# A two-layer vision tower on one core: three unsplit patch blocks, value rows torn 16, 16 and 5, and a reordered tail

## The reference

```python
h = patches @ W_lin.T + b_lin; h = concat(class_token, h) + position   # 768 -> 256
h = h + attention(layernorm(h))      # 16 heads of 64, softmax with a relative bias
h = h + moe(layernorm(h))            # 7 experts (256 -> 1024 -> 256), top 2, one shared expert
# last layer
d = sigmoid(x @ W_delta.T + b_delta); v = x @ W_value.T + b_value      # x = layernorm(h)
state = (1 - d) * state + d * v      # along the 37 tokens;  h = h + state
r = sigmoid(mix_r(x) @ W_r.T); k = square(relu(mix_k(x) @ W_k.T))      # x = layernorm(h)
h = h + r * (k @ W_v.T)              # mix: mu * x + (1 - mu) * previous token
```

## Time and profile before

| | us |
|---|---|
| median of three runs | 309.29 |
| the profiled execution | 307.67 |
| its span, first to last instruction | 305.6 |
| PE busy | 297.2 |
| DVE busy | 191.0 |
| ACT busy | 187.3 |
| POOL busy | 154.7 |

### The profile page before, as it was taken

The page is one execution under the profiler, slowest core; times in us unless marked ns, Lnnn a source line. Parts: engine busy times, 40 slices in busy tenths (PEclk is TensorE's granted clock), DMA queues, the critical chain, the costliest instruction groups (busy, mean ns, idle before and its releaser), DMA issues.

```text
span 305.6 us, 7417 instructions
## 1 busy us (share of the span) xinstructions
PE 297.2 (97%) x3100; PEld 277.3 (91%) x3100; DVE 191.0 (63%) x368; ACT 187.3 (61%) x327; POOL 154.7 (51%) x142
## 2 busy tenths in 40 slices
PE   8999998999999999989999999999999999998995
PEld 7778788999999999979999999999999999985673
DVE  2694445657727868675828674755748686736962
ACT  4586335776636883546777676657576463678561
POOL 7043523666415151729577594967685785000333
PEclk9999999999999999999999999999999999999999
DMA  7979343554604332478674838384857652000002
GB/s 267 412 161 233 67 113 94 182 143 124 194 8 135 82 111 72 166 214 283 228 216 151 252 124 288 96 290 135 274 170 233 207 186 73 11 4 1 0 0 84
DMA packets 32432, 46.49 MB, mean 152 GB/s; under 512 B 6965, under 2 KB 18837, under 8 KB 32394
## 3 DMA queue, kind: packets, MB, share of 16 engines
q1 hardware_dynamic: 29994, 42.16, 44.3%
q0 software_dynamic: 960, 2.43, 2.4%
q10 hardware_dynamic: 1440, 1.38, 1.5%
HBM read 38.22 MB, written 5.71 MB: 144 GB/s over the span
## 4 chain that ended last, share of the span: by engine, by line
PE 91%; DVE 4%; DMA 2%; ACT 1%; issue 1%; SPq 0%; ACTq 0%; POOL 0%; DVEq 0%; POOLq 0%
PE ps L1708 22%; PE ps L1710 22%; PE ps L1709 22%; PE ps L2098 6%; PE ps L1880 3%; PE ps L1723 3%; PE ps L1730 2%; PE ps L1860 2%; PE ps L1716 2%; DMA v_region<-v_region 2%; PE ps L1845 2%; PE ps L1738 1%; DVE c_region L1129 1%; PE ps L2009 1%; PE ps L1973 1%
## 5 line engine op out<-in xcount | busy, mean ns | idle before, releaser
L1708 PE MATMUL ps<-c_region,w_hi 128*128 128x224 f32 (+2 forms) x304 | 88.3, 290 | 1.1 <-DVE c_region L1129 0.8
L1710 PE MATMUL ps<-c_region,w_lo 128*128 128x224 f32 (+2 forms) x304 | 85.4, 281 | 0.0
L1709 PE MATMUL ps<-c_region,w_hi 128*128 128x224 f32 (+2 forms) x304 | 85.2, 280 | 0.0
L572 POOL TENSOR_TENSOR w_lo<-w_stage,w_hi 128x512 fp32r<-128x512 f32 x30 | 47.4, 1600 | 33.9 <-ACT w_hi L847 33.9
L1708 PEld LDWEIGHTS ps<-c_region,w_hi 128*128 128x128 f32 x304 | 58.1, 191 | 2.6 <-DVE c_region L1129 1.4
L1709 PEld LDWEIGHTS ps<-c_region,w_hi 128*128 128x128 f32 x304 | 58.1, 191 | 0.3
L1710 PEld LDWEIGHTS ps<-c_region,w_lo 128*128 128x128 f32 x304 | 58.0, 191 | 0.0
L847 ACT ACTIVATE w_hi<-w_stage 128x1024 fp32r<-128x1024 f32 (+1 forms) x41 | 47.7, 1177 | 2.2 <-DVE v_region L1553 2.2
L1129 DVE TENSOR_TENSOR c_region<-s_region,c_region 128x448 fp32r<-128x448 f32 (+1 forms) x44 | 38.6, 879 | 15.2 <-ACT c_region L979 12.3
L579 POOL TENSOR_TENSOR w_lo<-w_stage,w_hi 128x512 fp32r<-128x512 f32 x26 | 35.2, 1386 | 9.0 <-ACT w_hi L847 7.4
L1708 PE MATMUL ps<-xn_split,w_hi 128*128 128x296 f32 x128 | 39.4, 308 | 0.0
(11 more groups left out here) (183 smaller groups left out, 566.9 us busy)
## 6 DMA issues: line engine op xcount, KB each, us to landing
w_stage<-in_w_gate SPq DMA_DIRECT2D x17, 512.0 KB, 5.1
w_stage<-in_w_up SPq DMA_DIRECT2D x17, 512.0 KB, 4.6
w_stage<-in_w_down SPq DMA_DIRECT2D x7, 1024.0 KB, 5.6
expert_rows<-blank_rows SPq DMA_DIRECT2D x4, 448.0 KB, 3.6
v_region<-in_blocks SPq DMA_DIRECT2D x6, 272.0 KB, 3.8
w_stage<-in_w_down SPq DMA_DIRECT2D x3, 512.0 KB, 3.9
v_region<-expert_rows SPq DMA_DIRECT2D x1, 1344.0 KB, 8.5
expert_out<-v_region ACTq DMA_DIRECT2D x6, 224.0 KB, 3.5
```

What stands on the lines that cost most here:

```text
L572: w = g.tensor_tensor(wl[:, r], ws[:, r], wh[:, r].bitcast(F32), ALU.subtract)
L1708: mm(o, a_h, b_h, start=start, stop=False)
L1709: mm(o, a_h, b_l, start=False, stop=False)
L1710: return mm(o, a_l, b_h, start=False, stop=stop)
```

## The change

- `FULL` becomes 3: block 2 of the patch product is full in both halves, its ACT copies and DVE subtractions go, and so does one `patch_low` behind `centre(0, 0)`. In half c=1 both remaining full blocks, then `variance(0, 0)` and the bias product come ahead of the three split blocks.
- `GIVEN` becomes 16: the torn rows are 16, 16 and 5, and the groups have 111, 111, 127, 116 and 127 rows.
- `keep_clock` goes from 9 to 6 at the start, from 8 to 6 in the last layer, and away between values 2 and 3.
- Downs 6 and 7 of the shared expert move from behind `gate_up(8)` and `gate_up(9)` to behind `gate_up(10)` and `gate_up(11)`.
- In the last layer `mean(2, 1)` is issued one gate product earlier and `mean(3, 0)` one later; ACT's "one minus sigmoid" is a step of its own (`kept`) with a semaphore of its own, squares (2, 1) come ahead of `delta(0, 1)`, and squares (3, 0) ahead of the table load; DVE takes `normal(2, 1)` before `inject(0, 1)`.

```diff
@@ constants
-FULL = 2
+FULL = 3
...
-        GIVEN = P - 3 * T
+        GIVEN = 16
-        V_ROWS = (VR, VR, P, 3 * T + T - 2 * GIVEN, P)
+        V_ROWS = (VR, VR, VR + GIVEN, 3 * T + T - 2 * GIVEN, VR + GIVEN)
@@ scalar
                 a.activation(tmp[0][:, r], bank(4 + i, NC), ACT.Sigmoid,
                              bias=pb[:, PB_BD + m:PB_BD + m + 1]).then_inc(s["ra_sig"], 1)
-                act.wait_ge(s["ra_sig"], 2 * i + 1)
-                a.activation(tmp[2][:, r], tmp[0][:, r], ACT.Copy, scale=-1.0, bias=1.0).then_inc(s["ra_sig"], 1)
+
+            def kept(c, m):
...
+                act.wait_ge(s["ra_sig"], i + 1)
+                a.activation(tmp[2][:, r], tmp[0][:, r], ACT.Copy, scale=-1.0, bias=1.0).then_inc(s["ra_kept"], 1)
...
             delta(0, 0)
+            kept(0, 0)
+            square(2, 1)
             delta(0, 1)
-            square(2, 1)
             log_exp_tables()
             root(2, 1)
+            kept(0, 1)
             sigmoid_tables()
             delta(1, 0)
+            kept(1, 0)
             delta(1, 1)
+            kept(1, 1)
+            square(3, 0)
             log_exp_tables()
-            square(3, 0)
             root(3, 0)
@@ vector
             patch_low(FULL + 2, 1, SPLIT0 + 3)
-            patch_low(FULL + 3, 1, SPLIT0 + 4)
...
-                dve.wait_ge(s["ra_sig"], 2 * i + 2)
+                dve.wait_ge(s["ra_kept"], i + 1)
...
             add_state(0, 0, state(0, 0, inject(0, 0)))
-            in01 = inject(0, 1)
             normal(2, 1)
-            add_state(0, 1, state(0, 1, in01))
+            add_state(0, 1, state(0, 1, inject(0, 1)))
@@ tensor
-            keep_clock(9)
+            keep_clock(6)
...
-            embed(1, 1)
+            for k in range(1, FULL):
+                embed(k, 1)
+            variance(0, 0)
+            pe.wait_ge(s["d_bias_in"], 32)
+            mm(ps[0:HEADS, 5, 0:REL], tb[0:BUCKETS, :], cb[0:BUCKETS, CB_OH:CB_OH + REL],
+               start=True, stop=True).then_inc(s["bias_mm"], 1)
             for k in range(FULL, KF):
                 pe.wait_ge(s["tok_lo"], 2 * (KF - FULL) + k - FULL + 1)
                 embed(k, 1)
-                if k == FULL:
-                    variance(0, 0)
...
-                        keep_clock(9, 6, 16)
                         pe.wait_ge(s["d_xv"], 80)
...
-                if u < FRONT - 2:
+                if u < KH:
                     down(0, u - 2, first=u == 2)
+                if u >= FRONT - 2:
+                    down(0, u - 4)
...
                 gate(0, 0, 0)
+                mean(2, 1)
                 gate(0, 0, 1)
-                mean(2, 1)
                 gate(0, 1, 0)
                 variance(2, 1)
                 gate(0, 1, 1)
                 gate(1, 0, 0)
                 gate(1, 0, 1)
+                gate(1, 1, 0)
                 mean(3, 0)
-                gate(1, 1, 0)
                 gate(1, 1, 1)
                 variance(3, 0)
                 mean(3, 1)
-                keep_clock(8, 1)
+                keep_clock(6, 1)
```

More of the change, by code:

```diff
@@ L275, in vit_tower @@
             "weighted cbe_set hid_hi hid_lo dn_mm moe_mm ra_mm ra_sig "
-            "mix_mul mixr_mul mix_ok rk_mm r_sig k_relu k_sq vv_mm gated out_ok out0_ok").split()}
+            "ra_kept mix_mul mixr_mul mix_ok rk_mm r_sig k_relu k_sq vv_mm gated out_ok out0_ok").split()}
         d_patch = [sem(f"d_patch{i}") for i in range(KF)]
@@ L1067, in delta @@
                              bias=pb[:, PB_BD + m:PB_BD + m + 1]).then_inc(s["ra_sig"], 1)
-                act.wait_ge(s["ra_sig"], 2 * i + 1)
-                a.activation(tmp[2][:, r], tmp[0][:, r], ACT.Copy, scale=-1.0, bias=1.0).then_inc(s["ra_sig"], 1)
+            def kept(c, m):
+                i = KD * c + m
+                r = slice(m * N + c * NC, m * N + (c + 1) * NC)
+                act.wait_ge(s["ra_sig"], i + 1)
+                a.activation(tmp[2][:, r], tmp[0][:, r], ACT.Copy, scale=-1.0, bias=1.0).then_inc(s["ra_kept"], 1)
             def previous(c, m):
@@ L1760, in _ @@
                 embed(k, 1)
-                if k == FULL:
-                    variance(0, 0)
-                    pe.wait_ge(s["d_bias_in"], 32)
-                    mm(ps[0:HEADS, 5, 0:REL], tb[0:BUCKETS, :], cb[0:BUCKETS, CB_OH:CB_OH + REL],
-                       start=True, stop=True).then_inc(s["bias_mm"], 1)
             def value_full(g, n):
```

## The result

The changed kernel takes 306.63 us, the median of four runs from 305.40 to 306.86, against 309.53 us for the kernel before on the same chip (four runs, 309.12 to 311.34). The ratio is 0.9887, 95% interval 0.9839 to 0.9935. Three repeats beside other experiments gave 0.9906 (0.9879 to 0.9933), 0.9901 (0.9862 to 0.9939) and 0.9915 (0.9895 to 0.9936). Laid off from 309.29 us these are 305.8, 306.4, 306.2 and 306.7 us: the kernel is 2.6 to 3.5 us faster, where 2.35 was forecast. The profiled execution took 305.4 us, its span is 303.6.

A forecast was written before the change was run, and what follows sets the result against it. TensorE, busy 297.2 of 305.6 us, was taken as the bound. Terms -0.1 - 0.55 - 1.2 - 0.5 + 0 = -2.35 us, laid off from the median 309.29, gave 306.9 us, range 306.2 to 308.1.

The forecast's parts named there:

- Torn rows, -1.2 us: Before `contexts(1)`: with 16-row copies instead of 17, PE's whole DMA wait within v_region goes, -1.2 us.
- the lower end of -0.2: At the torn rows: if sixteen rows still went one by one, only about 0.2 us would be gained.
- The lower level as a rival: At the start: fewer zero blocks leave TensorE at 1.2 GHz through half c=0, +4.2 us, 311.1 us; 10% down to partial.
- the sign named for it: At the start: full patch matmuls 0.96 us apart after 5 us would show the forecast wrong.
- the prediction's condition for a harmless start: At the start: if the clock rises by 6.4 us, the pause ahead of block 3 absorbs nearly all.
- Zero blocks between the values, -0.55 us: Between values 2 and 3: the removed zero blocks held PE from 34.34 to 34.88, so -0.55 us.
- The thin cover: Between values 2 and 3: the gather lands by 34.3 us, where PE would arrive at 34.2; gain between 0 and -0.63.
- Start, -0.1 us: Patch product: half c=0 ends where it did, half c=1 changes between +0.2 and -0.3, taken as -0.1 us.
- Block 4: In half c=0 of the start: block 4's DMA and DVE low part set the pace; PE starts on it at 8.31.
- Shared expert, -0.5 us: After the last `gate_up`: PE goes on at 132.47 without idle time, -0.5 us, ends 0 and -0.55.
- collision: Shared expert: POOL's subtractions slow unit 9's DVE low part instead of unit 8's; rival that it only moves, 307.9 us, 10%.
- Last layer, 0 us: Last layer: earlier `mean(2, 1)` and later `mean(3, 0)` cancel in four steps, 0 us, ends -0.3 and +0.4.

The follow-up runs named there:

- e9_after_third: The changed kernel with nothing altered, timed again beside three other runs on one chip; 306.11 us.
- the 369.67 us execution: The profiled execution of the kernel before with only the last-layer edits; that run's median is 308.93 us, ratio 0.9998.

## Why the forecast was near, and where it was wrong

**Torn rows, -1.2 us: right in mechanism, too small in size.** The whole wait went, as taken, and the lower end of -0.2 is out (split 16 and 1). Timed it is -1.5 us twice, with intervals (-2.0 to -1.0, -2.2 to -0.8) that hold 1.2 as well. What the step left out is what the pause did afterwards. Over all jobs, kernels with the copy wait at `contexts(1)` fell to the lower clock in 28 of 190 executions (before 16 of 120), kernels without it in 1 of 105, and a fall costs about 2 us. That is 16/120 x 2.0 = 0.3 us of the kernel before's mean which the profiled execution, at 307.67 us quicker than the three timed runs beside it, could not show. Without the executions that fell, the means give -1.3 us for the torn rows alone and -1.0 for the split in 16 and 1, on either side of the 1.2 of the row. The prediction said of the clock that "in all of the rest the level never fell, and pauses of 1.2 us were among it". That sentence rested on one execution, and it is the step that failed: it put what follows the pause at nothing, and the runs show 0.3 us on the mean. Length alone does not bring a fall: waits and stalls of 1.2 us elsewhere (at the gather, and behind the 974th record with five tiny blocks more) stand in the profiled executions of two kernels that had 0 falls in 24. What decides is open.

**What is left of the distance.** Means without the falls have the changed kernel 2.4 to 2.7 us faster in its three repeats, against 2.35 forecast and 2.2 in the two traces; those last tenths have no cause that the runs show. The 3.5 us of the first comparison are in part luck: its fourth execution of the kernel before took 311.34 us, like one with a fall (its clock is not on record). The means give 0.9887 with it and 0.9903 without, and that is 306.3 us, within the range.

**The lower level as a rival.** At the start it was real, and little of it arrived. The first full patch matmuls do run at half rate: one takes 0.96 us instead of 0.48 until about 5.0 us in the result's own trace, until 6.1 in the run `e9_after_third` and until 6.6 with 17 rows, so the sign named for it (0.96 us apart after 5 us) did appear. The six full matmuls took 3.6 to 4.2 us in these three, waits aside, where 2.9 was forecast. The rise scatters by execution: with nine zero blocks it came at 4.1 us in the trace before, but at 6.1 in that of the torn rows alone. Here are the 17-row form, then PE's records in one microsecond, of the kernel before and of that form:

```profile
3.71 4.55 PE L1745 MATMUL ps<-v_region 128*128 128x288 f32 x12
5.00:6.00 1.00, 1.00 (x6) 1.00 0.98 370
5.00:6.00 1.00, 1.00 (x3) 1.00 1.02 390
```

(PE's busy time and records, granted clock, DMA share, GB/s. The granted clock reads 1.00 in both, so at the start the level is read from the distances.) The rise came by 6.6 at the latest, close to the 6.4 of the prediction's condition for a harmless start, and the two late ones reach the first value product at 18.08 and 18.20 us, within the scatter given below. The level was real again 45 us later, and there with the opposite sign for the change.

**Zero blocks between the values, -0.55 us: not borne out by the timings.** The trace gives the term, the timings do not: alone +1.4 us, with the torn rows 0, in the changed kernel undecided. The thin cover was named and its end of 0 kept; what was not named is that 18 records less move the issue stall, and that with the copy wait still there the clock falls more often (6 of 11 executions, and 4 of 12 with 17 rows in the changed kernel, against 16 of 120). Why the blocks make a fall rarer while the pause is still there was not tested further.

**Start, -0.1 us:** +0.06 in the trace, -0.5 to -0.3 timed with intervals that hold 0. Block 4 did not set the pace in every execution. In the first repeat of the changed kernel PE waited 1.1 us for block 3, for which ACT's wait for its DMA ended at 7.06 us instead of 6.20. From run to run this stage moves by up to 0.9 us (the first full value product starts between 17.73 and 18.64, FULL = 2 and the 369.67 us execution aside), the unchanged start included (17.73 to 18.44).

**Shared expert, -0.5 us:** as forecast in the trace, collision and all; timed within its wide interval.

**Last layer, 0 us: right sum, near in its steps, one price not seen.** Against `turn_rows(1)`, which came 2.25 us earlier, `gate(1, 0, 0)` moved by -0.7 (forecast -0.6), `centre(3, 0)` by +0.3 (forecast +0.4), the mixes by +0.1 (forecast +0.25) and the last products by -0.1. What the steps do not say is what the later `mean(3, 0)` costs by itself. Since `inject(1, 0)` stands behind `centre(3, 0)` on DVE's program, the mean put back brings the mixes and the last products 0.7 us forward. The later mean ate what the other edits of this stage gave.

**Sum.** The five parts run alone add to -0.9 us, the whole gives -2.6 to -3.5. Taking torn rows and blocks as the pair that was run (-1.5), the sum is -2.3; the distance to the whole is within the intervals. The +1.4 of the blocks alone needs the copy wait, and disappears with it.

## What to carry over

A wait on TensorE can cost more than its length: look at the granted clock of every execution, not only of the profiled one, before a pause is priced by its row. Where a forecast is laid off from a median, first ask what the median has that the profiled execution lacks. And a sum that comes out at nothing should be taken apart: here one edit cost the 0.7 us that the others gave, and undoing it gave the best kernel.

## What had not been expected of the hardware

- A pause of PE of 1.1 to 1.2 us can be followed, some 0.5 to 2 us after PE has gone on, by some 3.4 us at half the granted clock (51.0 to 54.4 us behind the copy, 74.3 to 77.7 us behind the issue stall). It follows in some executions and not in others of the same kernel.
- In streams of 37-column matmuls PE can stall for 0.1 to 1.2 us on its own issue. The place goes with the number of records ahead of it (973 or 974, and 126 more), so removing or adding work 30 to 60 us earlier moves it.
- One row more than 16 in an SBUF copy kept a DMA 5.3 us in flight; the same rows as 16 and 1 left a wait of 0.2 us.
- At the start the rise from half rate to full came between 4.1 and 6.6 us, by execution and not by the number of zero blocks, while the granted clock of those stretches reads 1.00.
